# Value projection of a 64-channel cross attention: three float32r products against one float32 product

## The chip, the cores and the metric

The kernel runs on one core of one Trainium2 chip. The metric is the device time of one execution in microseconds, taken as the median of several runs. The kernel is one program of twelve stages, run one after the other: four decoder layers, each with a self-attention-like stage, a cross attention and a feed-forward stage. The change touches one stage only, the cross attention of the second layer.

## The reference

Layer 1's cross attention takes the tokens `x` (8 batches of 100 tokens, 256 features) and the context `ctx_1024` (8 batches of 361 keys, 256 features). It has 16 heads of 64 channels, so queries, keys and values are 1024 wide:

```
q = x   @ Wq + bq        # 8 x 100 x 1024
k = ctx @ Wk + bk        # 8 x 361 x 1024
v = ctx @ Wv + bv        # 8 x 361 x 1024
p = softmax(q k^T / 8)   # per batch and head, 100 x 361
x = layernorm(x + (p v) @ Wo + bo)
```

All inputs are float32. The product that the change is about is `ctx @ Wv`: 361 rows by 256 by 1024 for each of the 8 batches.

## The kernel before

The stage is `wide_heads`. The 16 heads are taken in 8 pairs for each batch, 64 pairs in all, and the engines walk through them in slots: slot p computes the scores of pair p, turns the probabilities of pair p-2 and multiplies those of pair p-3 with the values. The order of the work on each engine is written out by hand, through a table `items` that places side jobs in the slots.

TensorE's order in slot p is: the scores of pair p (L1834, two heads side by side in the array); the turning of the probabilities of pair p-2 (L1843, six transposes); a value item, if the slot has one (L1809 to L1811); the product of probabilities and values of pair p-3 (L1856); then a query item (L1796), an output item (L1816) or the turning of the new x (L1821), where the slot has one. The scores of pair p+1 wait for the exponentials of pair p, since there is one score tile (PSUM banks 0 and 1).

VectorE's order in slot p is: the maximum of the scores (L1971), the copy of the even turned head (L1977), the reciprocal and the scaling (L1983, L1986), in seven slots `rest_of_context` (L1992), and then the copies out of PSUM of the side jobs (values L1959, queries L1951). ScalarE's is: two exponentials with their sums (L1898), the copy of the odd turned head (L1906), every fourth slot the copy of the outputs (L1912), in seven slots `cut_context` (L1917).

The values are projected in items. An item is half a width (512 columns, half of the heads of a batch) by a third of the keys (121, 121 or 119 rows). There are 48 items. Three stand before slot 0, behind the first four query items; the other 45 stand in slots 4h-2, 4h-1 and 4h for h = 1 to 15, so that three slots of four have one. The item's weights (the stationary operand) are rows of the context and its moving operand is a 512-column part of `Wv`. Both are cut into two parts whose sum is the float32 number: ScalarE writes the high part rounded to float32r, VectorE writes the rest. An item is then six float32r matmuls: for each of the two halves of the 256 features, low x high, high x high and high x low.

Context parts are made afresh for each batch, in a ring of two: `cut_context(j+1)` and `rest_of_context(j+1)` run in the slots p with p % 8 == 2, that is 2, 10, 18, 26, 34, 42 and 50. The first context and both halves of the weights are cut at the start of the stage. The context tiles have one spare column, so that an item reads 122 or 120 columns of them; GpSimd fills it at the start of the stage.

Of the kernel before, what the change touches and what calls it, by code (L numbers as in the profile page):

```python
# [9 lines left out]
F32R = mybir.dt.float32r  # L10
I32 = mybir.dt.int32
U8 = mybir.dt.uint8
ALU = mybir.AluOpType
ACT = mybir.ActivationFunctionType
AX = mybir.AxisListType

B, S, D = 8, 100, 256
KEYS = 361
P = 128
KT = D // P  # L20
TOK = B * S
KROWS = 121
# [1676 lines left out]
def wide_heads(nc, st, name, w, bias):  # L1699

    H, HD, PAIRS, T = 16, 64, 8, 3
    rows = [min(KROWS, KEYS - t * KROWS) for t in range(T)]
# [3 lines left out]
    VW = PER_HALF * P  # L1706
# [18 lines left out]
    with ExitStack() as ctx:  # L1725
        def sb(n, shape, dt=F32):
            return ctx.enter_context(nc.sbuf_tensor(f"{name}_{n}", shape, dt))
# [8 lines left out]
        rsum, rinv = sb("rsum", [S, 2, 2]), sb("rinv", [S, 2, 2])  # L1736
        o_norm = sb("o_norm", [P, 2, PAIRS * S])
        bias_rows = sb("bias_rows", [S, D])
        v_high, v_low = sb("v_high", [P, KT, PAIRS * P]), sb("v_low", [P, KT, PAIRS * P])
        x_high, x_low = sb("x_high", [P, 2, KT, KEYS + 1]), sb("x_low", [P, 2, KT, KEYS + 1])  # L1740
        r = lambda ap: ap.bitcast(F32R)

        sems = ["probs_set", "bias_made", "bias_ready", "x_biased", "q_ready", "q_copied", "v_ready", "v_copied",
                "scores_ready", "max_ready", "exp_done", "turned", "even_copied", "odd_copied", "values_done", "o_copied",
                "inv_ready", "scaled", "y_added", "spare_set", "v_high_set", "v_low_set", "x_high_set", "x_low_set",
                "k_loaded0", "k_loaded1", "k_loaded2", "k_loaded3"]
        with stage_sems(nc, sems + NORM_SEMS) as s, nc.Block(no_gpsimd_drain=True) as block:
            x_b = lambda j: st.X[:, j, :]
# [25 lines left out]

            @block.gpsimd
            def _(pool):
                pool.tensor_copy(r(x_high[:, :, :, KEYS]), st.head_mask[64].unsqueeze(1).to_broadcast([P, 2, KT])).then_inc(s.spare_set, 1)
                pool.tensor_copy(r(x_low[:, :, :, KEYS]), st.head_mask[64].unsqueeze(1).to_broadcast([P, 2, KT])).then_inc(s.spare_set, 1)
                pool.memset(probs[:], 0.0).then_inc(s.probs_set, 1)
                pool.wait_ge(s.bias_ready, 1)  # L1780
                for j in range(B):
                    pool.tensor_tensor(norm.resid[:, j, :], x_b(j), bias_rows[:], ALU.add).then_inc(s.x_biased, 1)
                for j in range(B):
                    rstd_pool(pool, norm, s, j)

            @block.tensor
            def _(pe):
                def on_the_side(x):
                    kind, n, part = x
                    bank = side_bank(x)  # L1790
                    wait_side(pe, x)
                    if kind == "q":
                        for i in range(2):
                            m = 2 * part + i
                            for k in range(KT):
                                last = pe.matmul(st.ps[:, bank, 2 * i * S:2 * (i + 1) * S], w.q[:, k, m * P:(m + 1) * P], st.XT[:, k, 2 * n:2 * n + 2, :],  # L1796
                                                 start=(k == 0), stop=(k == KT - 1))
                        last.then_inc(s.q_ready, 1)
                    elif kind == "v":
                        j, u = divmod(n, 2)  # L1800
                        wide = rows[part] + 1
                        at = slice(part * KROWS, part * KROWS + wide)
                        if n < 2 and part == 0:
                            pe.wait_ge(s.v_low_set, u + 1)
                        if u == 0 and part == 0:
                            pe.wait_ge(s.x_low_set, j + 1)
                        for k in range(KT):
                            high, low = r(v_high[:, k, u * VW:(u + 1) * VW]), r(v_low[:, k, u * VW:(u + 1) * VW])
                            pe.matmul(st.ps[0:wide, bank, 0:VW], r(x_low[:, j % 2, k, at]), high, start=(k == 0), stop=False)  # L1809
                            pe.matmul(st.ps[0:wide, bank, 0:VW], r(x_high[:, j % 2, k, at]), high, start=False, stop=False)  # L1810
                            last = pe.matmul(st.ps[0:wide, bank, 0:VW], r(x_high[:, j % 2, k, at]), low, start=False, stop=(k == KT - 1))  # L1811
                        last.then_inc(s.v_ready, 1)
                    elif kind == "y":
                        pe.wait_ge(s.o_copied, 2 * n + 2)
                        for m in range(PAIRS):
                            last = pe.matmul(st.ps[0:S, bank, 0:D], o_norm[:, n % 2, m * S:(m + 1) * S], w.o[:, m, :], start=(m == 0), stop=(m == PAIRS - 1))  # L1816
                        last.then_inc(s.y_ready, 1)
                    else:
                        pe.wait_ge(s.xnew_ready, n + 1)
                        for k in range(KT):  # L1820
                            last = pe.transpose(st.ps[:, bank, k * S:(k + 1) * S], st.X[:, n, k * P:(k + 1) * P], st.ident[0:S, 0:S])  # L1821
                        last.then_inc(s.xnew_turned, 1)
# [37 lines left out]
                for m in range(PAIRS):  # L1860
                    last = pe.matmul(st.ps[0:S, 0, 0:D], bias["v"][:, m:m + 1].to_broadcast([P, S]), w.o[:, m, :], start=(m == 0), stop=(m == PAIRS - 1))
# [18 lines left out]
            def _(act):  # L1880
# [30 lines left out]
                        act.wait_ge(s.y_ready, half // 2 - 1)  # L1911
                    act.activation(o_norm[:, half // 2 % 2, half % 2 * PER_HALF * S:(half % 2 + 1) * PER_HALF * S], o_tile, ACT.Copy).then_inc(s.o_copied, 1)  # L1912

                def cut_context(j):
                    if j >= 2:
                        act.wait_ge(s.v_ready, T * 2 * (j - 1))
                    act.activation(r(x_high[:, j % 2, :, 0:KEYS]), st.ctxT[:, j], ACT.Copy).then_inc(s.x_high_set, 1)  # L1917

                def cut_weights(high, w_all, u, done):
                    act.activation(r(high[:, :, u * VW:(u + 1) * VW]), w_all[:, :, u * VW:(u + 1) * VW], ACT.Copy).then_inc(done, 1)  # L1920

                act.wait_ge(s.spare_set, 2)
                cut_context(0)
                for u in range(2):
                    cut_weights(v_high, w.v, u, s.v_high_set)
                for x in front:
                    copy_out(x)
                for p in range(last_slot + 1):
                    if p < pairs:
                        exponentials(p)  # L1930
                    for x in items[p][0]:
                        copy_out(x)
                    if 0 <= p - 2 < pairs:
                        copy_turned(p - 2)
                    if 0 <= p - 3 < pairs and (p - 3) % PER_HALF == PER_HALF - 1:
                        copy_outputs((p - 3) // PER_HALF)
                    if p % PAIRS == 2 and p // PAIRS + 1 < B:
                        cut_context(p // PAIRS + 1)
                    for x in items[p][1] + items[p][2]:
                        copy_out(x)  # L1940

            @block.vector
            def _(dve):
# [41 lines left out]
                    for i in range(2):  # L1985
                        dve.tensor_scalar(probs[:, p % 3, i, 0:KEYS], probs[:, p % 3, i, 0:KEYS], rinv[:, p % 2, i:i + 1], None, ALU.mult).then_inc(s.scaled, 1)  # L1986

                def rest_of_context(j):
                    dve.wait_ge(s.x_high_set, j + 1)
                    if j >= 2:  # L1990
                        dve.wait_ge(s.v_ready, T * 2 * (j - 1))
                    dve.tensor_tensor(r(x_low[:, j % 2, :, 0:KEYS]), st.ctxT[:, j], x_high[:, j % 2, :, 0:KEYS], ALU.subtract).then_inc(s.x_low_set, 1)  # L1992

                def rest_of_weights(low, high, w_all, u, cut, done):
                    part = slice(u * VW, (u + 1) * VW)
                    dve.wait_ge(cut, u + 1)
                    dve.tensor_tensor(r(low[:, :, part]), w_all[:, :, part], high[:, :, part], ALU.subtract).then_inc(done, 1)

                rest_of_context(0)
                for u in range(2):  # L2000
                    rest_of_weights(v_low, v_high, w.v, u, s.v_high_set, s.v_low_set)
                dve.wait_ge(s.bias_made, 1)
                dve.tensor_tensor(bias_rows[:], st.ps[0:S, 0, 0:D], bias["o"][0:S, :], ALU.add).then_inc(s.bias_ready, 1)
                for x in front:
# [1 line left out]
                for p in range(last_slot + 1):  # L2006
                    if p < pairs:
                        maxima(p)
                    if 0 <= p - 2 < pairs:
                        copy_turned(p - 2)  # L2010
                    if 0 <= p - 1 < pairs:
                        scale(p - 1)
                    if p % PAIRS == 2 and p // PAIRS + 1 < B:
                        rest_of_context(p // PAIRS + 1)
                    for x in items[p][1] + items[p][2]:
                        copy_out(x)
                    if p % PAIRS == 6 and p > PAIRS:
                        normalise_vector(dve, norm, s, p // PAIRS - 1)
# [2197 lines left out]
def l1_xattn(nc, st, dram):  # L4216
    bias = scaled_query_bias(nc, st, "a4", 0.125)
    wide_heads(nc, st, "l1x", weights(st, "a4"), bias)
# [40 lines left out]
```

## Time and profile before

| | |
|---|---|
| Median of 3 runs | 2575.91 us (2573.95 to 2576.36) |
| The profiled execution, its own time | 2580.67 us |
| Its span, first to last instruction | 2578.9 us |
| Mean granted TensorE clock over the span | 0.885 |
| The stage `wide_heads` in the span | from 640.6 to 940.0 us |
| Slots 0 to 63 in the span | from 655.45 to about 929 us |

The span is counted from the first instruction; the own time has 1.8 us more around it. The profiled execution is 4.8 us longer than the median of the other runs. In the records of TensorE one float32 matmul shows as two records, and one float32r matmul as one.

### The profile page before, as it was taken

The numbers are of one execution on the slowest core, as the hardware profiler recorded it, in microseconds if no ns is written. First come the engines' busy times: TensorE is split into PE (matmuls) and PEld (weight loads), VectorE is DVE, ScalarE is ACT, GpSimd is POOL, SyncE is SP. The second block draws the span as 40 slices with busy tenths as digits, with TensorE's granted clock in tenths as the row PEclk, the third lists the DMA queues.
The fourth block names the chain that finished last, engine by engine and source line by source line (L and its number), as shares of the span: only waits on it lengthen the run. The fifth ranks groups of instructions, "written<-read, shape, count | busy, mean of one in ns | idle before, by whom it ended". The sixth has DMA issues, their size and how long they took to land. (4 is left out here: it accounts for less than half of the span.)

```text
span 2578.9 us, 42130 instructions
## 1 busy us (share of the span) xinstructions
PE 2173.7 (84%) x14706; PEld 1667.7 (65%) x14706; DVE 1572.4 (61%) x3629; ACT 1118.5 (43%) x3141; POOL 613.0 (24%) x725
## 2 busy tenths in 40 slices
PE   6799675888899976869978868979996899798994
PEld 4566443445666644659956537869995466598994
DVE  4566648997666653545555554546554455657886
ACT  5566345564343323533311444433332356454662
POOL 0200017996000010110022420000002322133555
PEclk9899787999999986669977979979997899798997
DMA  2000012432211114314310004322210000145772
GB/s 112 9 2 2 33 68 91 128 117 76 61 44 44 41 40 129 100 62 164 120 42 0 5 17 127 105 85 92 88 62 28 12 6 6 50 157 190 236 244 84
DMA packets 76679, 198.58 MB, mean 77 GB/s; under 512 B 20375, under 2 KB 46587, under 8 KB 74440
## 3 DMA queue, kind: packets, MB, share of 16 engines
q1 hardware_dynamic: 74444, 192.90, 23.2%
q0 software_dynamic: 2048, 3.29, 0.4%
q8 instruction: 106, 1.74, 0.3%
q14 instruction: 81, 0.66, 0.1%
HBM read 165.94 MB, written 30.21 MB: 76 GB/s over the span
## 5 line engine op out<-in xcount | busy, mean ns | idle before, releaser
L2421 PE MATMUL ps<-l1a_zc,tables_sb 128*128 128x400 f32 x256 | 113.9, 527 | 55.2 <-DVE l1a_zc L2386 27.6
L2349 POOL TENSOR_TENSOR l1a_dbx<-l1a_dx,l1a_rows 128x400 f32<-128x400 f32 x128 | 158.9, 1265 | 5.5 <-DMA l1a_rows<-l1a_rows_spilled 4.9
L1898 ACT ACTIVATE l1x_probs<-ps,l1x_nmax 100x361 f32<-100x361 f32 x128 | 70.8, 559 | 166.6 <-DVE l1x_nmax L1971 166.6
L2370 ACT ACTIVATE ps<-l1a_delta,weights 128x400 f32<-128x400 f32 x128 | 76.4, 597 | 80.2 <-DVE l1a_z_pool L2404 46.0
L2421 PEld LDWEIGHTS ps<-l1a_zc,tables_sb 128*128 128x128 f32 x256 | 46.5, 195 | 99.7 <-POOL l1a_zc L2338 48.4
L1026 ACT ACTIVATE l3x_probs<-l3x_s_sb,l3x_nmax 100x361 f32<-100x361 f32 x128 | 75.2, 589 | 70.3 <-DVE l3x_nmax L1115 66.3
L3045 PE MATMUL ps<-l3f_routed_x_high,l3f_routed_w_low 128*128 128x128 f32 x320 | 91.8, 287 | 15.4 <-DVE l3f_routed_w_low L3109 14.0
L2428 PE MATMUL ps<-ctxT,weights 128*128 128x361 f32 x256 | 100.5, 475 | 0.0
L1024 ACT ACTIVATE l0x_probs<-ps,l0x_nmax 100x361 f32<-100x361 f32 x128 | 70.8, 558 | 64.7 <-DVE l0x_nmax L1122 56.5
L2622 PE MATMUL ps<-l2f_x_high,l2f_w_high 128*128 128x400 f32 x272 | 95.0, 349 | 0.0
L2623 PE MATMUL ps<-l2f_x_low,l2f_w_high 128*128 128x400 f32 x272 | 94.4, 347 | 0.0
L2621 PE MATMUL ps<-l2f_x_high,l2f_w_low 128*128 128x400 f32 x272 | 94.3, 347 | 0.0
L2404 DVE TENSOR_TENSOR_SCAN l1a_z_dve<-ps,l1a_dbx 128x400 f32<-128x400 f32 x86 | 84.4, 983 | 14.8 <-POOL l1a_dbx L2349 9.9
L1115 DVE CUSTOM_DVE_ANT_0 l3x_s_sb<-ps,l3x_mask_b 100x361 f32<-100x361 f32 x128 | 63.2, 531 | 46.6 <-PE ps L931 46.3
L3046 PE MATMUL ps<-l3f_routed_x_high,l3f_routed_w_high 128*128 128x128 f32 x320 | 91.0, 284 | 0.0
L3047 PE MATMUL ps<-l3f_routed_x_low,l3f_routed_w_high 128*128 128x128 f32 x320 | 90.9, 284 | 0.0
L2778 DVE SCALAR_TENSOR_TENSOR l2f_hg<-ps,l2f_biases,l2f_act_out 128x800 f32<-128x800 f32 x34 | 35.7, 1051 | 72.5 <-PE ps L2623 72.5
L2386 DVE TENSOR_TENSOR l1a_zc<-l1a_z_dve,l1a_rows 128x400 f32<-128x400 f32 x86 | 79.8, 929 | 0.0
L1971 DVE TENSOR_REDUCE l1x_nmax<-ps 100x2 f32<-100x722 f32 x64 | 57.9, 905 | 34.4 <-PE ps L1834 34.2
L1399 PE MATMUL ps<-l2x_a_kept,l2x_a_taps 100*100 100x100 f32 x768 | 76.0, 258 | 2.7 <-DMA l2x_a_taps<-l2x_taps_spread 2.4
L1122 DVE TENSOR_REDUCE l0x_nmax<-ps 100x2 f32<-100x722 f32 x64 | 58.2, 909 | 32.3 <-PE ps L931 32.3
L1399 PEld LDWEIGHTS ps<-l2x_a_kept,l2x_a_taps 100*100 100x100 f32 x768 | 74.4, 174 | 5.2 <-DMA l2x_a_taps<-l2x_taps_spread 3.0
(708 smaller groups left out, 6617.5 us busy)
## 6 DMA issues: line engine op xcount, KB each, us to landing
ctxT<-l_ffn_units SPq DMA_DIRECT2D x20, 1026.0 KB, 5.7
l3f_expert<-l_ffn_units SPq DMA_DIRECT2D x20, 1026.0 KB, 5.9
l2x_a_taps<-l2x_taps_spread SPq DMA_DIRECT2D x8, 1912.5 KB
l2f_landing<-l_ffn_units SPq DMA_DIRECT2D x17, 771.0 KB, 4.3
l1a_rows<-l1a_rows_spilled SPq DMA_DIRECT2D x32, 400.0 KB, 3.6
l1f_gates<-l1f_gates SPq DMA_DIRECT2D x16, 800.0 KB, 4.1
l1x_keys<-l1a_key_sb SPq DMA_DIRECT2D x64, 180.5 KB, 2.4
l1x_kT<-l1x_keys SPq DMA_DIRECT2D x64, 180.5 KB, 2.3
```

The lines of the kernel that those rows point to most:

```text
L1399: last = pe.matmul(score_bank(r)[:, n, :], taps[:, j % 2, first:first + S], kept[:, g % 3, n, c:c + S], start=(c == 0), stop=(c == 2))
L2349: pool.tensor_tensor(dbx[:, n % BUFS, :], dx[:, j, m, :], rows[:, g % RING, 0, :], ALU.mult).then_inc(s.dbx_ready, 1)
L2386: dve.tensor_tensor(zc[:, n % DONE, :], z(n), rows[:, g % RING, 1, :], ALU.mult).then_inc(s.zc_dve, 1)
L2404: dve.tensor_tensor_scan(z(n), da(n), dbx[:, n % BUFS, :], 0.0, ALU.mult, ALU.add).then_inc(s.scan_done, 1)
L2421: pe.matmul(y_bank(m), st.ident, zc[:, n % DONE, :], start=(i == 0), stop=(i == NS - 1)).then_inc(s.sum_done, 1)
L2428: part = pe.matmul(key_bank(u), w_key[:, k, pair * P:(pair + 1) * P], st.ctxT[:, b, k, :], start=(k == 0), stop=(k == KT - 1))
L2621: pe.matmul(out, r(w_lo), r(x_hi), start=start, stop=False)
L2622: pe.matmul(out, r(w_hi), r(x_hi), start=False, stop=False)
L2623: return pe.matmul(out, r(w_hi), r(x_lo), start=False, stop=stop)
L3045: pe.matmul(out, r(lo), r(x_high[i % 2][:, k, :]), start=(k == 0), stop=False)
L3046: pe.matmul(out, r(hi), r(x_high[i % 2][:, k, :]), start=False, stop=False)
L3047: last = pe.matmul(out, r(hi), r(x_low[i % 2][:, k, :]), start=False, stop=(k == KT - 1))
```

## The change

The values are projected straight from the float32 context `st.ctxT` and the float32 weights `w.v`. An item becomes two float32 matmuls (one for each half of the 256 features) in place of six float32r ones, of 121 or 119 weight columns. The cutting of the context on ScalarE and VectorE, the cutting of the weights, the spare columns on GpSimd, the four buffers of parts (`v_high`, `v_low`, `x_high`, `x_low`) and five semaphores are gone. Everything else keeps its place in the order.

```
-        v_high, v_low = sb("v_high", [P, KT, PAIRS * P]), sb("v_low", [P, KT, PAIRS * P])
-        x_high, x_low = sb("x_high", [P, 2, KT, KEYS + 1]), sb("x_low", [P, 2, KT, KEYS + 1])
...
             def _(pool):
-                pool.tensor_copy(r(x_high[:, :, :, KEYS]), ...).then_inc(s.spare_set, 1)
-                pool.tensor_copy(r(x_low[:, :, :, KEYS]), ...).then_inc(s.spare_set, 1)
...
                     elif kind == "v":
                         j, u = divmod(n, 2)
-                        wide = rows[part] + 1
-                        at = slice(part * KROWS, part * KROWS + wide)
-                        if n < 2 and part == 0:
-                            pe.wait_ge(s.v_low_set, u + 1)
-                        if u == 0 and part == 0:
-                            pe.wait_ge(s.x_low_set, j + 1)
+                        at = slice(part * KROWS, part * KROWS + rows[part])
                         for k in range(KT):
-                            high, low = r(v_high[:, k, u * VW:(u + 1) * VW]), r(v_low[:, k, u * VW:(u + 1) * VW])
-                            pe.matmul(st.ps[0:wide, bank, 0:VW], r(x_low[:, j % 2, k, at]), high, start=(k == 0), stop=False)
-                            pe.matmul(st.ps[0:wide, bank, 0:VW], r(x_high[:, j % 2, k, at]), high, start=False, stop=False)
-                            last = pe.matmul(st.ps[0:wide, bank, 0:VW], r(x_high[:, j % 2, k, at]), low, start=False, stop=(k == KT - 1))
+                            last = pe.matmul(st.ps[0:rows[part], bank, 0:VW], st.ctxT[:, j, k, at], w.v[:, k, u * VW:(u + 1) * VW], start=(k == 0), stop=(k == KT - 1))
                         last.then_inc(s.v_ready, 1)
...
-                act.wait_ge(s.spare_set, 2)
-                cut_context(0)
-                for u in range(2):
-                    cut_weights(v_high, w.v, u, s.v_high_set)
...
-                    if p % PAIRS == 2 and p // PAIRS + 1 < B:
-                        cut_context(p // PAIRS + 1)
...
-                rest_of_context(0)
-                for u in range(2):
-                    rest_of_weights(v_low, v_high, w.v, u, s.v_high_set, s.v_low_set)
...
-                    if p % PAIRS == 2 and p // PAIRS + 1 < B:
-                        rest_of_context(p // PAIRS + 1)
```

## Rows read from the trace of the kernel before

**Rows 1.** The page's busy time of TensorE over the whole span.

```profile
PE 2173.7 (84%) x14706; PEld 1667.7 (65%) x14706; DVE 1572.4 (61%) x3629; ACT 1118.5 (43%) x3141; POOL 613.0 (24%) x725
```

**Rows 2.** Windows of the stage: length, busy us of each engine, granted clock.

```profile
640.00:655.40 15.40, 14.80 (x66) 12.28 (x66) 7.55 (x11) 2.70 (x3) 7.70 (x11) 0.89 0.51 183
655.40:669.20 13.80, 9.14 (x29) 4.40 (x28) 7.01 (x13) 4.59 (x14) 0.00 (x0) 0.63 0.15 41
669.20:926.00 256.80, 244.27 (x1804) 167.30 (x1804) 173.75 (x390) 103.85 (x327) 5.46 (x14) 1.00 0.16 42
```

**Rows 3.** TensorE's waits, 655 to 940 us: total us, times, longest.

```profile
PE ps L1834 <- ACT l1x_probs L1898: 17.2, 17, 2.3
```

**Rows 4.** Timeline of TensorE, slot 18, with a value item: start, length.

```profile
731.86 0.88 PE L1843 MATMUL ps<-tables_sb,l1x_probs 100*121 100x100 f32 x6
732.51 0.47 PE L1809 MATMUL ps<-l1x_v_high,l1x_x_low 128*122 128x512 f32 x1
732.83 0.39 PE L1810 MATMUL ps<-l1x_v_high,l1x_x_high 128*122 128x512 f32 x1
...
734.08 0.74 PE L1856 MATMUL ps<-l1x_probsT,l1x_vals 121*64 121x100 f32 x12
734.75 0.55 PE L1834 MATMUL ps<-l1x_kT,l1x_qT 64*100 64x361 f32 x2
```

**Rows 5.** Timeline of TensorE, slot 5, without a side job.

```profile
676.56 0.88 PE L1843 MATMUL ps<-tables_sb,l1x_probs 100*121 100x100 f32 x6
677.37 0.74 PE L1856 MATMUL ps<-l1x_probsT,l1x_vals 121*64 121x100 f32 x12
678.97 0.85 PE L1834 MATMUL ps<-l1x_kT,l1x_qT 64*100 64x361 f32 x4 [0.86 <-ACT l1x_probs L1898]
```

**Rows 6.** Timeline of TensorE in the stage before, dense float32 at full clock.

```profile
422.18 0.83 PE L2421 MATMUL ps<-l1a_zc,tables_sb 128*128 128x400 f32 x2
422.85 0.77 PE L2428 MATMUL ps<-ctxT,weights 128*128 128x361 f32 x2
423.46 0.83 PE L2421 MATMUL ps<-l1a_zc,tables_sb 128*128 128x400 f32 x2
```

**Rows 7.** Groups of TensorE in the stage, shapes apart: count, busy us, mean ns.

```profile
L1816 PE MATMUL ps<-weights,l1x_o_norm 128*100 128x256 f32 x128 | 29.6, 384 | 0.7 <-ACT l1x_o_norm L1912 0.7
L1809 PE MATMUL ps<-l1x_v_high,l1x_x_low 128*122 128x512 f32 x64 | 28.4, 443 | 0.0
...
L1809 PE MATMUL ps<-l1x_v_high,l1x_x_low 128*120 128x512 f32 x32 | 13.8, 431 | 0.0
```

**Rows 8.** Timeline of all engines in slot 19, after a slot with cutting.

```profile
735.26 0.80 ACT L1917 ACTIVATE l1x_x_high<-ctxT 128x722 fp32r<-128x722 f32 x1
...
736.09 0.91 DVE L1992 TENSOR_TENSOR l1x_x_low<-ctxT,l1x_x_high 128x722 fp32r<-128x722 f32 x1 [2.01 <-ACT l1x_x_high L1917]
...
736.92 0.69 DVE L1959 COPY l1x_vals<-ps 121x512 f32<-121x512 f32 x1
...
737.52 0.90 DVE L1971 TENSOR_REDUCE l1x_nmax<-ps 100x2 f32<-100x722 f32 x1
...
739.80 0.85 PE L1834 MATMUL ps<-l1x_kT,l1x_qT 64*100 64x361 f32 x4 [1.31 <-ACT l1x_probs L1898]
```

**Rows 9.** Timeline of TensorE: the scores of slots 11 and 12.

```profile
698.37 0.85 PE L1834 MATMUL ps<-l1x_kT,l1x_qT 64*100 64x361 f32 x4
...
702.35 0.85 PE L1834 MATMUL ps<-l1x_kT,l1x_qT 64*100 64x361 f32 x4 [0.23 <-ACT l1x_probs L1898]
```

**Rows 10.** Timeline of TensorE: first value item before slot 0, first scores.

```profile
651.07 0.53 PE L1809 MATMUL ps<-l1x_v_high,l1x_x_low 128*122 128x512 f32 x1
...
655.45 0.85 PE L1834 MATMUL ps<-l1x_kT,l1x_qT 64*100 64x361 f32 x4
```

**Rows 11.** Timeline of TensorE: the value item of slot 2, scores of slot 3.

```profile
664.98 0.77 PE L1809 MATMUL ps<-l1x_v_high,l1x_x_low 128*122 128x512 f32 x1
...
667.81 1.49 PE L1834 MATMUL ps<-l1x_kT,l1x_qT 64*100 64x361 f32 x4
```

More of the change, by code:

```diff
@@ L1738, in wide_heads @@
         bias_rows = sb("bias_rows", [S, D])
-        v_high, v_low = sb("v_high", [P, KT, PAIRS * P]), sb("v_low", [P, KT, PAIRS * P])
-        x_high, x_low = sb("x_high", [P, 2, KT, KEYS + 1]), sb("x_low", [P, 2, KT, KEYS + 1])
-        r = lambda ap: ap.bitcast(F32R)
         sems = ["probs_set", "bias_made", "bias_ready", "x_biased", "q_ready", "q_copied", "v_ready", "v_copied",
                 "scores_ready", "max_ready", "exp_done", "turned", "even_copied", "odd_copied", "values_done", "o_copied",
-                "inv_ready", "scaled", "y_added", "spare_set", "v_high_set", "v_low_set", "x_high_set", "x_low_set",
+                "inv_ready", "scaled", "y_added",
                 "k_loaded0", "k_loaded1", "k_loaded2", "k_loaded3"]
@@ L1776, in _ @@
             def _(pool):
-                pool.tensor_copy(r(x_high[:, :, :, KEYS]), st.head_mask[64].unsqueeze(1).to_broadcast([P, 2, KT])).then_inc(s.spare_set, 1)
-                pool.tensor_copy(r(x_low[:, :, :, KEYS]), st.head_mask[64].unsqueeze(1).to_broadcast([P, 2, KT])).then_inc(s.spare_set, 1)
                 pool.memset(probs[:], 0.0).then_inc(s.probs_set, 1)
@@ L1912, in copy_outputs @@
                     act.activation(o_norm[:, half // 2 % 2, half % 2 * PER_HALF * S:(half % 2 + 1) * PER_HALF * S], o_tile, ACT.Copy).then_inc(s.o_copied, 1)
[L1914 to L1920, printed above, removed]
-                act.wait_ge(s.spare_set, 2)
-                cut_context(0)
-                for u in range(2):
-                    cut_weights(v_high, w.v, u, s.v_high_set)
                 for x in front:
@@ L1986, in scale @@
                         dve.tensor_scalar(probs[:, p % 3, i, 0:KEYS], probs[:, p % 3, i, 0:KEYS], rinv[:, p % 2, i:i + 1], None, ALU.mult).then_inc(s.scaled, 1)
[L1988 to L1997, printed above, removed]
-                rest_of_context(0)
-                for u in range(2):
-                    rest_of_weights(v_low, v_high, w.v, u, s.v_high_set, s.v_low_set)
                 dve.wait_ge(s.bias_made, 1)
```

## The prediction

> **What bounds the kernel now.** The page's busy times come first: TensorE is busy for 84% of the span [rows 1]. That is a mean over twelve stages, so next come the windows of this stage. From 669.2 to 926 us TensorE is busy for 244.27 of 256.80 us, at full clock (2.4 GHz) throughout, with VectorE at 68% and ScalarE at 40%; before that lie 13.8 us that begin and end at full clock but are mostly at 1.2 GHz, mean 0.63 [rows 2]. Then the waits: all that TensorE loses between 655 and 940 us is 17 waits of its scores for the exponentials, 17.2 us [rows 3]. So the stage has two limits that take turns by slot. One is TensorE's own queue. The other is the chain of one pair: scores, maximum, two exponentials, next scores.
>
> The timeline tells which slot has which. In a slot without a side job TensorE sits idle for 0.86 us before the next scores [rows 5]: the chain ends last. Slot 5 goes from 675.78 to 678.97, so that the chain alone takes 3.19 us and TensorE's own work 2.33 us. In a slot with a value item the next scores start with no idle time before them (734.75 after 731.08, 3.67 us) [rows 4]: TensorE ends last. All 45 slots with a value item are of this kind, but for those that follow the cutting of a context. There, at slot 19, the next scores stand idle for 1.31 us [rows 8]; in slot 11 for 0.23 us [rows 9]. I read the same two patterns three times each: slots 19, 35 and 51 take 5.05 us, and slots 11, 27 and 43 take 3.98 us, where slots with a value item and nothing else take 3.67.
>
> **The item on TensorE.** It loses six float32r matmuls and gains two float32 ones.
>
> Old price: from the turning (731.86) to the value item is 0.65 us, from the item to the product with the values 1.57 us, together 2.22 [rows 4]. Without the item the turning and that product are 0.81 us apart (676.56 to 677.37) [rows 5]. The item costs 2.22 - 0.81 = 1.41 us. Within it a float32r record of 512 columns takes at most 4.38 / 18 = 0.243 us with both ends of a run of 18 counted [rows 10], and 0.23 without them, which is near one column per cycle.
>
> New price: no float32 matmul of 512 columns stands in the trace, but the same operand types stand with 361 and 400 columns. Two records of 400 columns take 422.85 - 422.18 = 0.67 us and two of 361 take 423.46 - 422.85 = 0.61 us [rows 6], so 0.336 and 0.304 us a record. Both are 0.833 ns a column (two cycles) and 2.5 ns beside. A float32 matmul is two records: the 64 matmuls of the output items (8 batches by 8) show as 128 records, while the 96 matmuls of the first product of the value items show as 64 + 32 = 96 [rows 7]. A 512-column record is then 0.427 + 0.0025 = 0.429 us, the item four of them, 1.716 us. In rows 6 one line follows another with nothing between, and context columns are the weights in both old and new items, so I add nothing for the entrance. The item gets 1.716 - 1.41 = 0.31 us longer.
>
> The bounds: an output item, placed between tiles of another form, costs 0.17 us beside its records (3.63 us for 16 of 0.216). If the value item pays that too it is +0.48. At the low end, four time stamps read to 0.01 us leave +0.27.
>
> The Trainium skill's page "FP8 and Floating Point Precision", section "TensorE Precision Notes", says that true FP32 makes four passes through the array; the trace agrees, with two records of two cycles a column against one record at one cycle. Counting four passes at the 0.23 us of a float32r record would make the item 1.85 us, +0.44 us, and the sum below 6 us larger; rows 6 speak for 0.429 a record, so I keep 0.31.
>
> **Where it lies on the path.** In the 45 slots TensorE ends last, so each of them grows by 0.31 us: 45 x 0.31 = 13.95 us. What hides nothing here might elsewhere: the slots without an item keep 0.86 us of idle TensorE time, but they hold none of the new work. VectorE's copy of the values (L1959) and the next maximum move with the item; both start from the end of TensorE's work and keep their distance.
>
> **Before slot 0.** Three items follow each other, from 651.07 to 655.45, 4.38 us [rows 10]. New: twelve records of 0.429 = 5.15 us, 0.09 us to the scores, and an entrance 0.06 us later: 5.30. That is +0.92 us, and slot 0 starts that much later. Cutting the weights and the first context ends at 645.2 us, behind the bias product that TensorE runs until 645.8, so taking it away brings nothing.
>
> **At 1.2 GHz.** The item of slot 2 runs at half clock: 664.98 to 667.81 is 2.83 us, of which six records of 0.427 are 2.56 [rows 11]. New: four of 0.853 = 3.41 and the same 0.27, so 3.68, +0.85. That is 0.54 us above the 0.31 that I counted.
>
> **The cutting that goes.** In slot 18 ScalarE cuts the next context from 735.26, VectorE subtracts from 736.09, then copies the values, and only at 737.52 takes the maximum of slot 19, whose scores began at 734.75 [rows 8]. In an undisturbed slot that maximum starts 0.9 us after the scores, here 2.77. The 1.87 us make the slot 5.05 us. Without the cutting VectorE has the copy done before the scores are, and the slot falls back on TensorE's 3.66 us: 1.39 us back, three times, 4.17 us. In slots 11, 27 and 43 a query item on TensorE covers most of the delay; 3.98 us is almost exactly the new length of such a slot (3.97), so 0.31 us comes back in each, 0.93 us. After slot 2 the maximum waited for the scores alone, so nothing. The copies by GpSimd at the start are no one's wait.
>
> **Sum.** 13.95 + 0.92 + 0.54 - 4.17 - 0.93 = +10.3 us. The profiled execution's own 2580.67 us becomes 2591.0. It lies 4.76 us above the median of the runs; the same difference gives 2575.91 + 10.3 = 2586.2 us, +0.4%.
>
> **Rivals.**
> 1. The clock stays low longer. The low stretch ends at 669.2, just as slot 3's second half begins. If slot 0 starts 0.92 us later and the clock rises only after slot 3, its item takes 3.43 us and not 1.72, and the product behind it 1.3 and not 0.67: +2.3, 2588.5 us. For it: the front is longer. Against it: TensorE is also busy longer before its idle time, which can shift the fall. Chance 0.17.
> 2. Every item pays the change of form or a fourth pass at full float32r price: +0.44 to +0.48 an item, 45 x 0.15 = 6.8 us more, 2593 us. Against it rows 6, where entrances are free. Chance 0.08.
> 3. Later stages shift. Their clock falls and rises several dozen times; moved by 10 us against those steps, they may give or take 3 us: 2583 to 2589 around the sum. The three runs of before lie within 2.4 us of each other, so this is mostly inside my range. Chance 0.08 that it goes beyond 2.5 us.
> 4. The other side: the chain, not TensorE, holds the slots with an item, the longer item hides, and only the cutting shows. Then the stage loses 4.17 + 0.93 + 0 and gains only 1.5: 2572.3 us. It decides from the point where TensorE's work in such a slot is below 3.19 - 0.31 = 2.88 us; it is 3.67 [rows 4], with no idle time. Chance 0.02.
> 5. A float32 record of 512 columns runs at one cycle a column: four of 0.216 = 0.86 us an item, 0.55 less than now, of which 0.48 shows before the chain's 3.19 us ends last: 45 x 0.48 + 5 = 27 us off, 2549 us. The Trainium skill, "TensorE: Matmul & The Clock Gate", section "Back-to-back issue gap", even gives about 131 ns a matmul of 512 columns for a sustained stream; the float32r records of this stage are 0.23 us apart, so the trace does not agree. Rows 6 and 7 speak against this rival. Chance 0.01.
>
> **How the numbers follow.** My forecast has 0.64, by itself 2583.5 to 2588.5 us (item +0.27 to +0.35, 1.8 us either way, and the median's own 1 us). Rival 1 reaches 2589, rival 3 both 2583 and 2590; the range 2582 to 2591.5 leaves out rivals 2, 4 and 5 and the tails. Within 0.2% (5.2 us, about what a measurement of this kernel tells from no change) is 2570.8 to 2581.1: the low tail of rival 3 and rival 4 with a loss of its own, 0.05. Faster by more is rival 5 and the rest of 4: 0.02. Slower: 0.93.
>
> **What the profile after would show.** The value item as one line with 4 records per item, 192 in all, of about 0.593 us each at full clock (0.427 and the 0.166 by which the 400-column records outlast their columns), 0.43 us apart. Slots with an item 3.97 to 3.98 us; slots 19, 35 and 51 no longer 5.05; the waits for the exponentials down from 17.2 us by 3 x 1.31 + 3 x 0.23 = 4.6 us. The scores of slot 0 at 656.4. The prediction is wrong if the records lie more than 0.44 us apart, if slots with an item show idle time before the next scores, or if the windows at 1.2 GHz before slot 4 are longer or shorter than 10 us.

## The result, and the profile after

| | before | after |
|---|---|---|
| Median, 7 runs each | 2575.18 us (2571.22 to 2576.36) | 2584.84 us (2581.54 to 2587.33) |
| Profiled execution, own time | 2580.67 us | 2581.54 us |
| Its span | 2578.9 us | 2579.7 us |
| Mean granted clock | 0.885 | 0.891 |

The changed kernel is slower by 9.7 us: the ratio of its runs to those of before is 1.0037, with a 95% interval of 1.0025 to 1.0048. The forecast was 10.3 us more, at 2586.2 us. One execution of before, among those that belong to the experiments below, took 2869.5 us at a mean granted clock of 0.705, where the others of its series had 0.886 to 0.891; it is in no median and no ratio here.

The two profiled executions differ by only 0.9 us, which is not the size of the change: the one of after is the fastest of its seven runs and the one of before is slower than all seven. The stage itself has to be read. Below are the windows of the stage after: length, busy us of each engine, granted clock.

```profile
640.00:654.60 14.60, 14.20 (x62) 10.25 (x62) 4.11 (x7) 0.00 (x0) 7.43 (x9) 1.00 0.53 193
654.60:670.50 15.90, 11.24 (x49) 5.33 (x48) 8.75 (x18) 5.41 (x18) 0.00 (x0) 0.79 0.18 48
670.50:933.00 262.50, 254.58 (x1694) 149.11 (x1693) 167.86 (x379) 97.94 (x316) 5.48 (x14) 1.00 0.15 41
```

They answer to [rows 2]. The last of them starts at slot 4, and not in slot 3 as that of [rows 2]; the clock itself was back at full at 665.7 us, before slot 3 began, where in the trace of before it was back at 669.1, within slot 3. So the two long windows, 256.8 and 262.5 us, don't hold the same slots. From the scores of slot 4 to those of slot 63 (672.11 to 925.70 us in the timeline of before, 670.51 to 932.93 after) it is 253.6 us before and 262.4 after: +8.8 us. ScalarE and VectorE are less busy and TensorE is busier.

TensorE's waits for the exponentials from 655 to 940 us, to be held against [rows 3]:

```profile
PE ps L1821 <- ACT l1x_probs L1885: 12.6, 11, 2.3
```

Six waits and 4.6 us are gone, as forecast. TensorE's timeline of slots 19 and 20:

```profile
736.43 0.85 PE L1821 MATMUL ps<-l1x_kT,l1x_qT 64*100 64x361 f32 x4
737.22 0.88 PE L1830 MATMUL ps<-tables_sb,l1x_probs 100*121 100x100 f32 x6
737.93 1.90 PE L1798 MATMUL ps<-weights,ctxT 128*121 128x512 f32 x4
739.76 0.74 PE L1843 MATMUL ps<-l1x_probsT,l1x_vals 121*64 121x100 f32 x12
740.43 0.85 PE L1821 MATMUL ps<-l1x_kT,l1x_qT 64*100 64x361 f32 x4
```

Slot 19 takes 740.43 - 736.43 = 4.00 us, where it took 5.05 [rows 8], and no idle time stands before the next scores. From the turning to the product with the values it is 739.76 - 737.22 = 2.54 us, where it was 2.22 [rows 4] and 0.81 without an item [rows 5]. The item costs 1.73 us in place of 1.41. Slot 11 keeps its length: 4.00 us without idle time against 3.98 with 0.23 of it [rows 9].

```profile
698.41 0.85 PE L1821 MATMUL ps<-l1x_kT,l1x_qT 64*100 64x361 f32 x4
...
702.41 0.85 PE L1821 MATMUL ps<-l1x_kT,l1x_qT 64*100 64x361 f32 x4
```

VectorE's timeline in slot 19 after:

```profile
736.62 0.69 DVE L1932 COPY l1x_vals<-ps 121x512 f32<-121x512 f32 x1 [1.17 <-PE ps L1843]
737.33 0.91 DVE L1944 TENSOR_REDUCE l1x_nmax<-ps 100x2 f32<-100x722 f32 x1
```

The maximum starts 0.90 us after the scores, where it started 2.77 us after them [rows 8].

The groups of the value item, shapes apart, hold 192 records. Their means include the records at 1.2 GHz before slot 4; the median record is 0.592 us long, where 0.593 was forecast. Below are the groups, and then the start of the stage in TensorE's timeline.

```profile
L1798 PE MATMUL ps<-weights,ctxT 128*121 128x512 f32 x128 | 61.6, 605 | 0.0
L1798 PE MATMUL ps<-weights,ctxT 128*119 128x512 f32 x64 | 30.4, 597 | 0.0
```

```profile
640.40 3.67 PE L1848 MATMUL ps<-weights 128*100 128x256 f32 x16 [1.53 <-PEq L4187]
643.91 5.58 PE L1791 MATMUL ps<-XT,weights 128*128 128x200 f32 x32
649.32 5.31 PE L1798 MATMUL ps<-weights,ctxT 128*121 128x512 f32 x12
654.57 0.85 PE L1821 MATMUL ps<-l1x_kT,l1x_qT 64*100 64x361 f32 x4
```

The three items before slot 0 take 654.57 - 649.32 = 5.25 us, 0.87 more than the 4.38 of before [rows 10]. In this execution the bias product ahead of them ran at full clock.

### The profile page after: what moved, and what is told of

The parts are those of the page before. It is cut to its first block and busy times, and to the rows that moved or that the text cites. A ratio compares the mean times of both kernels' runs of the same rounds, so it can differ in the third digit from the quotient of the medians.

```text
span 2579.7 us, 41901 instructions
## 1 busy us (share of the span) xinstructions
PE 2177.6 (84%) x14610; PEld 1643.0 (64%) x14610; DVE 1565.8 (61%) x3619; ACT 1111.4 (43%) x3131; POOL 614.0 (24%) x723
## 5 line engine op out<-in xcount | busy, mean ns | idle before, releaser
L1798 PE MATMUL ps<-weights,ctxT 128*121 128x512 f32 (+1 forms) x192 | 91.7, 602 | 0.0
```

The costliest lines, as they stand in the source:

```text
L1798: last = pe.matmul(st.ps[0:rows[part], bank, 0:VW], st.ctxT[:, j, k, at], w.v[:, k, u * VW:(u + 1) * VW], start=(k == 0), stop=(k == KT - 1))
```

## The experiments

My theory: in each slot either TensorE's queue or the chain of scores, maximum and exponentials ends last. The item adds about 0.32 us to each slot where the queue does, and the cutting had held the chain back in six slots. The rivals: the longer items hide behind the chain; the cutting costs in every place, or in none; only TensorE's total of work counts. The first four runs below share a series, with before at 2574.7 us (median of 14 runs); the last four share another on another chip, with before at 2577.20 us (23 runs). A ratio is always to the before of the same series, and the medians of the last four lines of the table, too, are to be held against 2577.2.

Slot lengths, in us, read as differences of the starts of the scores in the timelines. "Item alone" are the slots with a value item that have no other side job and follow none (4, 6, 7, 8, 18, 20, 22 and so on to 60). "Slots 4 to 63" is the time from the scores of slot 4 to those of slot 63. Each column is constant within 0.06 us over the slots that it names, but for three kinds: slots that gave away half an item (3.18 to 3.19), slots 22, 38 and 54 of half_the_product (3.39, not looked into), and slot 36 of rest_of_context_twice (5.20, see there).

| kernel | item alone | 19, 35, 51 | 11, 27, 43 | slots 4 to 63 | median |
|---|---|---|---|---|---|
| before | 3.67 | 5.05 | 3.98 | 253.6 | 2575.2 |
| after | 4.00 | 4.00 | 4.00 | 262.4 | 2584.8 |
| after_again | 4.00 | 4.00 | 4.00 | 262.4 | 2586.1 |
| no_later_cutting | 3.67 | 3.67 | 3.68 | 248.4 | 2567.0 |
| float32_with_cutting | 4.00 | 5.05 | 4.00 | 265.6 | 2591.7 |
| cutting_in_slot_5 | 3.67 | 3.67 | 3.68 | 248.5 | 2567.5 |
| half_items_moved_f32r | 3.67 | 3.67 | 3.68 | 243.8 | 2567.3 |
| half_items_moved_f32 | 4.00 | 4.00 | 4.00 | 255.7 | 2580.1 |
| half_the_product | 3.18 | 3.18 | 3.18 | 227.1 | 2545.2 |
| rest_of_context_twice | 3.67 | 5.99 | 4.92 | 260.6 | 2584.4 |

**The changed kernel again** (after_again), unaltered.

> The changed kernel once more, unaltered. My account: +10.3 us on before, of which each of the 45 slots with a value item has +0.31 to +0.33 (4.00 us a slot), and slots 19, 35 and 51 are 4.00 us and not 5.05. Its profile shows whether the half-clock stretch near slots 0 to 3 comes out shorter than before's (as in the first profile of the changed kernel) or varies from one execution to the next.

Ratio 1.0038 (1.0023 to 1.0053), 2586.13 us. The slots repeat the first profile to 0.01 us in sum. What differed is the start: from the first instruction of the stage to the scores of slot 0 it took 15.8 us here and 14.1 in the first profile, because the bias product ran partly at 1.2 GHz this time. The half-clock stretch of slots 1 and 2 was 6.8 us long in both profiles.

**No cutting after the first context** (no_later_cutting). All contexts use the parts of context 0, and the wait for the parts of each context goes with the cutting.

```
-                    if p % PAIRS == 2 and p // PAIRS + 1 < B:
-                        cut_context(p // PAIRS + 1)
...
-                        rest_of_context(p // PAIRS + 1)
...
-                            pe.matmul(..., r(x_low[:, j % 2, k, at]), high, ...)
+                            pe.matmul(..., r(x_low[:, 0, k, at]), high, ...)
...
```

> The kernel before with its float32r items, but all contexts use the parts of context 0, so the seven later cuttings (ScalarE and VectorE) are left out; the values of contexts 1 to 7 are therefore those of context 0. My account: slots 19, 35, 51 fall from 5.05 to 3.67 us and slots 11, 27, 43 from 3.98 to 3.67: 5.1 us faster than before, about 2570. Rival, that the cutting costs in all seven places (1.87 us each): 13 us faster. Rival, that cutting was hidden: no change.

Ratio 0.9970 (0.9959 to 0.9982), 2566.97 us, 7.7 us below before; in slots 4 to 63 it is 5.2 us. The six slots fell to 3.67 to 3.70 as expected, and none of the others from slot 4 on moved by more than 0.04 us. The slot sum carries the verdict: 5.2 us, in six places, not in seven and not 13 us. The remaining 2.5 us of the medians lie outside those slots, and 5.2 us is within the interval of the ratio (4.6 to 10.6 us).

**Float32 items with the cutting kept** (float32_with_cutting).

```
+                        at = slice(part * KROWS, part * KROWS + rows[part])
                         for k in range(KT):
-                            (three float32r matmuls)
+                            last = pe.matmul(st.ps[0:rows[part], bank, 0:VW], st.ctxT[:, j, k, at], w.v[:, k, u * VW:(u + 1) * VW], start=(k == 0), stop=(k == KT - 1))
```

> The float32 items of the change, with all the cutting of before kept (its parts are written and used by nothing). My account: 42 slots grow by 0.31 to 0.33 us, slots 19, 35, 51 stay at 5.05 (the cutting still ends last there) and slots 11, 27, 43 stay at about 4.0: with +0.92 before slot 0 and +0.54 at half clock it is 39 x 0.32 + 1.5 = 14 us slower than before, 3.3 to 4.2 us slower than the changed kernel. Rival, that the items hide behind the chain of scores, maximum and exponentials: not above +2 us.

Ratio 1.0049 (1.0032 to 1.0066), 2591.70 us. Slots 4 to 63 are 12.0 us longer than before and 3.15 us longer than after. TensorE's timeline of slots 18 and 19:

```profile
735.38 0.85 PE L1832 MATMUL ps<-l1x_kT,l1x_qT 64*100 64x361 f32 x4
736.17 0.88 PE L1841 MATMUL ps<-tables_sb,l1x_probs 100*121 100x100 f32 x6
736.88 1.90 PE L1809 MATMUL ps<-weights,ctxT 128*121 128x512 f32 x4
738.71 0.74 PE L1854 MATMUL ps<-l1x_probsT,l1x_vals 121*64 121x100 f32 x12
740.43 0.85 PE L1832 MATMUL ps<-l1x_kT,l1x_qT 64*100 64x361 f32 x4 [0.98 <-ACT l1x_probs L1896]
```

The slot is 5.05 us long with either item; only the idle time before the next scores has fallen, from 1.31 [rows 8] to 0.98 us. In these three slots the longer item is hidden, as my theory has it, and in slots 11, 27 and 43 all but 0.02 us of it; in the other slots with an item it is not.

**The cutting moved to slots with an output item** (cutting_in_slot_5), float32r items.

```
-                    if p % PAIRS == 2 and p // PAIRS + 1 < B:
+                    if p % PAIRS == (2 if p < PAIRS else 5) and p // PAIRS + 1 < B:
                         cut_context(p // PAIRS + 1)
...
-                    if p % PAIRS == 2 and p // PAIRS + 1 < B:
+                    if p % PAIRS == (2 if p < PAIRS else 5) and p // PAIRS + 1 < B:
                         rest_of_context(p // PAIRS + 1)
```

> The kernel before with its float32r items; contexts 2 to 7 are cut in slots p % 8 == 5 and not 2, beside the output item that keeps TensorE busy for 3.6 us. My account: the delay of the next maximum is covered there, so slots 19, 35, 51 fall to 3.67 and 11, 27, 43 too: 5 us faster than before and 14 to 15 us faster than the changed kernel, about 2570. Rival, that the cutting delays a maximum wherever it stands: no change against before.

Ratio 0.9972 (0.9958 to 0.9985), 2567.54 us. Slots 4 to 63 are 5.1 us shorter, the same as without any later cutting. The timeline of slot 13 shows where it lies now:

```profile
708.47 3.70 PE L1816 MATMUL ps<-weights,l1x_o_norm 128*100 128x256 f32 x16
709.44 0.81 ACT L1917 ACTIVATE l1x_x_high<-ctxT 128x722 fp32r<-128x722 f32 x1
710.29 0.91 DVE L1992 TENSOR_TENSOR l1x_x_low<-ctxT,l1x_x_high 128x722 fp32r<-128x722 f32 x1 [1.06 <-ACT l1x_x_high L1917]
...
712.09 0.85 PE L1834 MATMUL ps<-l1x_kT,l1x_qT 64*100 64x361 f32 x4
```

Both parts of the cutting end at 711.2 us, before TensorE has done its output item. The cost of the cutting was one of place. Context 1 is still cut in slot 2, as before.

**Half items moved, float32r** (half_items_moved_f32r), on top of the last one. The matmuls for k = 1 of the last item of halves 1, 2, 4, ..., 14 run one slot later, where no item stands.

```
-            items[PER_HALF * half - 2 + t][1].append(("v", half, t))
+            later = t == 2 and (half == 1 or half % 2 == 0)
+            items[PER_HALF * half - 2 + t + later][1].append(("v", half, t))
...
                     for x in items[p][1]:
-                        on_the_side(x)
+                        on_the_side(x, (1,) if x in halved else range(KT))
+                    for x in items[p + 1][1]:
+                        if x in halved:
+                            on_the_side(x, (0,))
```

> The kernel before with float32r items, contexts 2 to 7 cut in slots p % 8 == 5, and in addition the second half (k = 1) of the last item of 8 of the 15 groups moved into the slot without an item behind it (slots 5, 9, 17, 25, 33, 41, 49, 57), which has 0.86 us of idle TensorE time. My account, TensorE's queue and the pair's chain take turns by slot: the slots 4, 8, 24, 40, 56 fall from 3.67 to the chain's 3.19, slots 16, 32, 48 (with a query item) from 5.22 to 4.53, and the receiving slots stay at 3.19: 4.5 us below the kernel that only moves the cutting, 9.6 below before, about 2565. Rival, that the stage is simply TensorE's total work: no change, since no work goes.

Ratio 0.9959 (0.9941 to 0.9976), 2567.26 against 2577.20 us in its own series: 9.9 us below before and, by the slots, 4.7 below the last one (4.5 expected). By the slots it is the fastest version that computes the whole reference; by the ratios alone it can't be told from the last one, whose interval overlaps its own. TensorE's timeline of slots 8 and 9:

```profile
687.12 0.85 PE L1838 MATMUL ps<-l1x_kT,l1x_qT 64*100 64x361 f32 x4
...
688.56 0.48 PE L1812 MATMUL ps<-l1x_v_high,l1x_x_low 128*120 128x512 f32 x1
...
689.43 0.74 PE L1860 MATMUL ps<-l1x_probsT,l1x_vals 121*64 121x100 f32 x12
690.31 0.85 PE L1838 MATMUL ps<-l1x_kT,l1x_qT 64*100 64x361 f32 x4
...
691.75 0.48 PE L1812 MATMUL ps<-l1x_v_high,l1x_x_low 128*120 128x512 f32 x1
...
693.49 0.85 PE L1838 MATMUL ps<-l1x_kT,l1x_qT 64*100 64x361 f32 x4
```

Slot 8 fell from 3.67 to 3.19 us and slot 9 stayed at 3.18 with its new half item. In slot 8 TensorE's own work ends at 690.17 and the scores start at 690.31 us, so the chain ends last there, by 0.14 us; where an item is whole, the scores start before the end of the last product. Slots 16, 32 and 48 fell from 5.21 to 4.52. TensorE does the same work as before the move, so total work is not what sets the time.

**Half items moved, float32** (half_items_moved_f32), the same edit on the changed kernel.

> The changed kernel (float32 items) with the same eight half items moved. My account: slots 4, 8, 24, 40, 56 fall from 4.00 to 3.19 us, slots 16, 32, 48 from 5.55 to 4.69, receiving slots at 3.19 to 3.25: 6.6 us faster than the changed kernel, 3 to 4 us slower than before. Rival, total work decides: no change against the changed kernel.

Ratio to before 1.0010 (0.9999 to 1.0022), 2580.10 against 2577.20 us: by the medians it can't be told from before, and by the slots it is 2.2 us slower. Slots 4 to 63 are 6.7 us shorter than in the changed kernel (6.6 expected), and the receiving slots take 3.17 to 3.19 us. So the spread of the work gives back three quarters of the 8.8 us that the change cost there. That is not the whole of the comparison: with the cutting and the half items moved, the float32r kernel needs 243.8 us for the same slots, 11.9 us less.

**Half of the product left out** (half_the_product). The accumulation then ends with k = 0 (its `stop` is changed with it).

```
-                        for k in range(KT):
+                        for k in range(KT if n == 0 else 1):
...
```

> The changed kernel, but items 1 to 15 of the halves leave out the second half of the 256 features (only k = 0 is multiplied), so an item is two float32 records. My account: an item falls by 0.86 us; slots with an item alone end at the chain's 3.19 us (0.81 less than 4.00), those with a query item too at 4.69 (0.86 less): about 36 us faster than the changed kernel. Rival, items are hidden already: no change. Rival, a float32 record of 512 columns costs only one cycle a column: half of that.

Ratio 0.9885 (0.9864 to 0.9906), 2545.16 us; slots 4 to 63 are 35.3 us shorter than after. TensorE's timeline of one slot with an item (two records):

```profile
674.06 0.85 PE L1821 MATMUL ps<-l1x_kT,l1x_qT 64*100 64x361 f32 x4 [0.84 <-ACT l1x_probs L1885]
...
675.55 1.04 PE L1798 MATMUL ps<-weights,ctxT 128*121 128x512 f32 x2
...
677.23 0.85 PE L1821 MATMUL ps<-l1x_kT,l1x_qT 64*100 64x361 f32 x4
```

3.17 us, which is the chain's length. TensorE's own work in such a slot is 4.00 - 0.86 = 3.14 us, nearly the same, so this run alone would not show that the chain is the floor; the slots with half a float32r item do. With a query item it is 4.69, 0.85 less than the 5.54 of after, which is the price of two records, and not the half of it that one cycle a column would give.

**The subtraction twice** (rest_of_context_twice).

```
+                    if j > 0:
+                        dve.tensor_tensor(r(x_low[:, j % 2, :, 0:KEYS]), st.ctxT[:, j], x_high[:, j % 2, :, 0:KEYS], ALU.subtract).then_inc(s.x_twice, 1)
+                        dve.wait_ge(s.x_twice, j)
```

> The kernel before, with VectorE's subtraction for contexts 1 to 7 made twice, one after the other. My account: it lies ahead of the next maximum on VectorE, so slots 19, 35, 51 grow by 0.9 to 1.0 us each (5.05 to 6.0) and slots 11, 27, 43 by the same (3.98 to 4.9): 5.5 to 6 us slower than before. Rival, ScalarE's part sets the delay and VectorE's is hidden: no change.

Ratio 1.0026 (1.0012 to 1.0040), 2584.35 us. VectorE's timeline and the scores that wait, slot 19:

```profile
737.22 0.91 DVE L1993 TENSOR_TENSOR l1x_x_low<-ctxT,l1x_x_high 128x722 fp32r<-128x722 f32 x1 [2.01 <-ACT l1x_x_high L1917]
738.17 0.91 DVE L1995 TENSOR_TENSOR l1x_x_low<-ctxT,l1x_x_high 128x722 fp32r<-128x722 f32 x1
738.99 0.69 DVE L1959 COPY l1x_vals<-ps 121x512 f32<-121x512 f32 x1
739.60 0.90 DVE L1971 TENSOR_REDUCE l1x_nmax<-ps 100x2 f32<-100x722 f32 x1
```

```profile
735.88 0.85 PE L1834 MATMUL ps<-l1x_kT,l1x_qT 64*100 64x361 f32 x4
...
741.87 0.85 PE L1834 MATMUL ps<-l1x_kT,l1x_qT 64*100 64x361 f32 x4 [2.26 <-ACT l1x_probs L1898]
```

All six slots grew by 0.94 to 0.95 us, 5.6 us in sum, one for one with the second subtraction. The sum of the slots grew by 7.1: one more slot (36, from 814.47 to 819.66 us) took 5.20 us and not 3.66. The window and the value item there show why:

```profile
815.80:819.30 3.50, 3.50 (x16) 2.40 (x16) 1.98 (x6) 1.51 (x5) 0.00 (x0) 0.52 0.21 53
```

```profile
817.02 0.63 PE L1811 MATMUL ps<-l1x_v_low,l1x_x_high 128*120 128x512 f32 x1
817.45 0.63 PE L1809 MATMUL ps<-l1x_v_high,l1x_x_low 128*120 128x512 f32 x1
```

The granted clock was 0.52 and the records stand 0.43 us apart in place of 0.23: TensorE ran at 1.2 GHz for 3.4 us, after 147 us at full clock and 2.25 us of idle time before the scores of slot 36. The same idle time stands before slots 20 and 52, where the clock stayed up. So the longer wait may have a part in the fall, but one execution doesn't show it.

## Why the prediction held, step by step

- **The item, +0.31 us a slot.** Measured +0.32 to +0.33 (1.73 against 1.41 us; slots of 4.00 against 3.67, where 3.97 to 3.98 was forecast). A float32 record of 512 columns was priced from those of 361 and 400 columns at 0.429 us; four make 1.716, and the entrance from the transposes costs 0.02 more. The rival of a dear entrance or a dear fourth pass (+0.44 to +0.48) is out. The Trainium skill's page "FP8 and Floating Point Precision", section "TensorE Precision Notes", counts four passes for true FP32. The records agree in number (two of two cycles a column), while the time of a pass, 0.215 us, is below the 0.23 us of a float32r record.
- **In 45 slots.** Shown: each slot with an item after slot 3 grew by 0.29 to 0.35 us, except the six that follow a slot with cutting. The half items moved show the point where it stops, the chain's 3.18 us, and half the product agrees. The rival that the items hide is out.
- **The cutting, -5.1 us.** Measured -5.2 and -5.1 by leaving it out and by moving it, and 3 x 1.05 = 3.15 us between the float32 items with and without it. As to its mechanism, the doubled subtraction shows that VectorE's part lies ahead of the maximum. VectorE had stood idle for 2.01 us for ScalarE's part before it [rows 8], so ScalarE should have a share in the delay too; no run changed ScalarE's part alone.
- **Slots 4 to 63 together.** Forecast 43 x 0.31 - 5.1 = +8.2 us, measured +8.8: 43 x 0.01 to 0.02 too little for the item.
- **Before slot 0, +0.92 us.** The items took 5.25 us, +0.87. From the stage's first instruction to slot 0 it was 14.8 us in five of five profiles with float32r items. With float32 items it was 15.8 in three and 14.1 in two, where the bias product ran at full clock throughout. With part of the bias product at 1.2 GHz on both sides it is thus +1.0, near the forecast, but in the profile of after it was 0.7 us less than before. Whether the change has a part in that is open.
- **At 1.2 GHz, +0.85 us for slot 2.** Too much in most executions: slot 2 took 5.53 us before and 5.59, 5.83, 5.82 and 6.00 us in the four profiles with whole float32 items, +0.06 to +0.47, since the clock rose within the slot. Slots 2 and 3 together, forecast at 2 x 0.31 + 0.54 = +1.16, take 9.59 to 10.00 us with float32 items, where three profiles with float32r items and an equally long slow stretch have 9.52 to 9.65: between 0 and +0.5.
- **The sum, +10.3 us.** The stage by its parts is +8.8 in slots 4 to 63, +1.0 before slot 0 and 0 to +0.5 in slots 2 and 3, together 9.8 to 10.3 us where the clock is alike; the medians say 9.7, with an interval from 6.4 to 12.4. The mechanism was right, but that the sum is so close is partly luck: 0.6 us too little for the items at full clock and 0.7 to 1.2 us too much for slots 2 and 3 cancel.
- **The clock stays low longer** (first rival). It did not: the stretch near slots 0 to 3 was 6.8 us long in all five profiles with float32 items, and 10.2 us in two of five with float32r items. The profile of before has the long one, which is one reason why its span is not 8.8 us shorter than the one of after: slots 0 to 3 took 16.7 us in it and 15.9 in after. A slow stretch before slot 4 that is shorter than 10 us was named as a sign that the prediction is wrong. That sign came, at 6.8 us; the forecast of the clock was wrong there, by 0.7 us of time, and the item and the chain were not touched by it. The scores of slot 0 came at 654.57 us and not at 656.4 for the reason given above.
- **Later stages.** The layer 1 feed-forward stage that follows took between 361.0 and 369.2 us in the ten profiles, first instruction to first instruction of the next stage, with no change to it (369.2 before, 365.6 after). Its time goes roughly with the mean granted clock in it, from 0.76 in the longest to 0.80 in the shortest. The rest is hardly steadier: the stages ahead of this one, also unchanged, end between 637.5 and 645.3 us, and those behind the feed-forward stage spread over 4.7 us. So single executions differ by about as much as the change is worth, and only the medians, and the slots, can carry it.

## What to carry to other kernels

Find for each slot of a hand-written order which of two limits ends last, from the idle time before the one instruction where they meet; then price an edit only in the slots where its engine ends last. A price for a shape that the trace lacks can be had from the same kind of record at two other widths, through the distance of the starts and not the length of the records. Before cutting into parts is given up for being costly on the helpers, ask whether it only stands in the wrong slot: here one condition, edited on both helper engines, won 5 us where the float32 products lost 9 to 10.

## What the runs showed beyond that

At 2.4 GHz a float32 record of 512 columns follows another at 0.43 us: (654.57 - 649.32) / 12 = 0.44 with both ends, and leaving two records out took 0.86 us from a slot (5.55 to 4.69). A float32 product of 512 columns, 0.86 us, therefore takes 0.17 us longer than three float32r products of 0.23. A matmul group may stay open in its PSUM bank for the length of a slot (from 688.56 to 691.75 us), with matmuls into other banks between, at no cost that the slots show: in the half items moved, slot 9 kept its 3.18 us.
